# Adding and gating y in a selective scan: from GpSimd to VectorE, in halves

## The chip, the cores and the metric

The kernel runs on one core of a Trainium2 chip. Its engines are TensorE (PE; its weight loads are PEld), VectorE (DVE), ScalarE (ACT), GpSimd (POOL) and SyncE (SP, which only issues DMAs here). Each engine runs its own list of instructions in order, and waits on semaphores that other instructions raise. The metric is the device time of one launch in microseconds, as the median of several runs.

## The reference, cut to what matters

A block of a language model on 2048 tokens of width 512. The tokens are normalised, and the result goes through a Mamba2 scan and, beside it, through a top-2 mixture of eight experts; both are added to the input. What the change touches is the end of the scan:

```python
Y_off = jnp.einsum('bclgn,bcgHpn,bgHcl->bclgHp', Cc, prev, jnp.exp(dA_cs))
y = (Y_diag + Y_off).reshape(b, l, NHEADS, HEADDIM) + x * D_skip[None, None, :, None]
y = y.reshape(b, l, D_INNER)
y = y * jax.nn.silu(z)
yg = y.reshape(b, l, NGROUPS, D_INNER // NGROUPS)
yg = yg * jax.lax.rsqrt(jnp.mean(yg * yg, axis=-1, keepdims=True) + EPS)
y = yg.reshape(b, l, D_INNER) * norm_w
return y @ out_proj_w.T
```

`Y_diag` is what a tile of tokens gives itself, `Y_off` what the carried state gives it. `z` comes from the input projection, as `x`, `B` and `C` do (these through a convolution over four tokens).

## The kernel before

The scan works on T = 16 tiles of 128 tokens. The input projection works on G = 8 groups of two tiles and is cut into nine pairs of 128 columns (`stage(g, n)`), five that go through the convolution and four that make z. While the tiles t = 2g and 2g + 1 are scanned, the stages of group g + 1 are computed: four of them in the even tile, five in the odd one, placed by hand between the steps of the scan in the lists of TensorE, ScalarE and VectorE. All queues are written out by hand; what sets the order is the text of each engine's function, and semaphores tie them.

The steps that matter here, with the lines of the profile:

- TensorE, in a tile t: turns x into the banks `pxb` (L1601, behind `cadd`, the end of the adding of the states), a `stage`, C times B (L1608), in odd tiles `router(g + 2)` (L1438 to L1448), which computes scores and time steps of the group after next into bank `pxb[0]`, and so waits for `xdt_done` of the tile it stands in (L1442); a `stage`, `join`, then `project(t - 1)`, the output product of the tile before (L1523); then `off` (L1579, the carried state's part), `squares`, `diag` (L1586, the tile's own part), `states` (L1570), and further stages. A `stage` waits until the bank of the pair two stages before is free (`pair_free`).
- VectorE: xdt (L1282) from `pxb`, C times B masked (L1287), the decay kernel m (L1304), the convolution (L972) and its gate (L987), `decayed` (L1245: e2 becomes the carried part of y), `own` (L1255: y is the tile's own part and the skip), `carried` (L1275: the states are added to the carry), in even tiles `finish` (L1021: the output row), and the zs step (L978) of the z pairs, which also frees the pair's bank. The stages that are left at the end of a tile's list stand behind `carried` (L1363 to L1375). The zs step waits for ScalarE's tanh, and this for TensorE's stage.
- GpSimd: xdd (L516, from xdt), `sums` of the squares (L499 to L503), the decay of the carry (L528), `factor` (L508), and then for y of tiles 0 to 13: y plus e2 (L535, raises `yadd`; not in tile 0) and y times zs (L538, raises `ygate`), each over the whole tile, 128 partitions x 1024.
- In tiles 14 and 15 VectorE adds and gates y itself, in halves of 512 columns, inside `own` (L1259 to L1268, with `last_add` and `last_gate`).
- Who waits for `yadd`: SP's load of the next e2 (`load_decays2`). Who waits for `ygate`: TensorE's `project` and ScalarE's squares (L710).

The routing to the experts is computed in tiles 12 to 15 on VectorE (`choose`, `place_of`, `probabilities`, tables), and the experts follow the scan, from about 500 us on.

Of the kernel before, what the change touches and what calls it, by code (L numbers as in the profile page):

```python
# [11 lines left out]
ALU = mybir.AluOpType  # L12
# [9 lines left out]
P = 128  # L22
# [7 lines left out]
T = TOKENS // P  # L30
# [32 lines left out]
NX, NZ = CB // 2, XB // 2  # L63
# [34 lines left out]
def need(eng, semaphore, n):  # L98
    if n > 0:
        eng.wait_ge(semaphore, n)  # L100
# [21 lines left out]
def block(nc, x, w_in, w_dtr, w_out, conv_w_in, conv_b_in, dt_bias, a_log, d_skip_in, norm_w_in, w_gu, w_down, ident_in,  # L122
          tri_in, row_in, part_in, sel_in, tab_in, out):
    with ExitStack() as ctx:
        def sem(name):
            return ctx.enter_context(nc.semaphore(name))
# [51 lines left out]
        zs = [sb("zs0", [P, XB, GT])]  # L178
# [5 lines left out]
        y = sb("y", [P, XB, P])  # L184
# [8 lines left out]
        e2 = sb("e2", [P, XB, P])  # L193
# [92 lines left out]
        in_full, inx_free, inz_free, tz_done = sem("in_full"), sem("inx_free"), sem("inz_free"), sem("tz_done")  # L286
# [6 lines left out]
        e2_done, cbt, cbm_done, m_done, xdd_done = sem("e2_done"), sem("cbt"), sem("cbm_done"), sem("m_done"), sem("xdd_done")  # L293
        st, yoff, ydiag, ye, yd = sem("st"), sem("yoff"), sem("ydiag"), sem("ye"), sem("yd")
        cdec, cadd, yadd, ygate = sem("cdec"), sem("cadd"), sem("yadd"), sem("ygate")
        last_add, last_gate, ysqd, tree = sem("last_add"), sem("last_gate"), sem("ysqd"), sem("tree")
        op, ss, var_done, rstd_done = sem("op"), sem("ss"), sem("var_done"), sem("rstd_done")
        o_done, o_out, last_out = sem("o_done"), sem("o_out"), sem("last_out")

# [43 lines left out]
        def heads(vec, c):  # L343
            return vec[c][:, :].rearrange("p (a b) -> p b a", a=2).unsqueeze(3).broadcast_to([P, XB, 2, HD])
# [9 lines left out]
        def sync(sp):  # L354
# [18 lines left out]
                sp.dma_start(m[t % 2][:, :, :], cs_d[t].unsqueeze(0).broadcast_to([P, HEADS, P])).then_inc(bc_in[t % 2], 16)  # L373

            def load_decays2(t):
                if t < T - 1:
                    need(sp, yadd, t - 1)
                else:
                    sp.wait_ge(last_add, 2)
                for half in range(2):  # L380
                    sp.dma_start(e2[half * HD:(half + 1) * HD, :, :],
                                 cs_d[t][half * XB:(half + 1) * XB, :].unsqueeze(0).broadcast_to([HD, XB, P])
                                 ).then_inc(e2_in, 16)
# [37 lines left out]
            for t in range(T):  # L421
                g, c = t // 2, t % 2
# [57 lines left out]
        def gpsimd(pool):  # L480
            def root(q):
                pool.wait_ge(veps_done, q + 1)
                pool.tensor_tensor(rstdx[:, :], veps[:, :], nhalf[:, :], ALU.pow).then_inc(rstdx_done, 1)
# [13 lines left out]
            def sums(t):  # L497
                pool.wait_ge(ysqd, t + 1)
                pool.tensor_tensor(ysq[:, 0:4, :], ysq[:, 0:4, :], ysq[:, 4:8, :], ALU.add).then_inc(tree, 1)  # L499
                pool.wait_ge(tree, t * 3 + 1)  # L500
                pool.tensor_tensor(ysq[:, 0:2, :], ysq[:, 0:2, :], ysq[:, 2:4, :], ALU.add).then_inc(tree, 1)
                pool.wait_ge(tree, t * 3 + 2)
                pool.tensor_tensor(ysq[:, 0:1, :], ysq[:, 0:1, :], ysq[:, 1:2, :], ALU.add).then_inc(tree, 1)  # L503
# [6 lines left out]
            for t in range(T):  # L510
                g, c = t // 2, t % 2
                if t < T - 1:
                    pool.wait_ge(xdt_done, 2 * t + 2)
                    pool.wait_ge(dec_done, t + 1)
                    need(pool, st, t)
                    pool.tensor_tensor(xdd[:, :, :, :], xdt[:, :, :, :], heads(dec, c), ALU.mult).then_inc(xdd_done, 1)  # L516
                if c == 0 and g + 2 < G:
                    root(g + 2)
                if 0 < t < T - 2:
                    sums(t - 1)  # L520
                if t == T - 1:
                    factor(t - 1)
                if t == T - 1:
                    break
                if t:
                    pool.wait_ge(yoff, 2 * t)
                    pool.wait_ge(cadd, 2 * t)
                    pool.tensor_tensor(carry[:, :, :, :], carry[:, :, :, :], heads(cd, c), ALU.mult).then_inc(cdec, 1)  # L528
                    factor(t - 1)
                if t == T - 2:  # L530
                    continue
                pool.wait_ge(yd, 2 * t + 2)
                if t:
                    pool.wait_ge(ye, 2 * t)
                    pool.tensor_tensor(y[:, :, :], y[:, :, :], e2[:, :, :], ALU.add).then_inc(yadd, 1)  # L535
                    pool.wait_ge(yadd, t)
                pool.wait_ge(inz_free, NZ * (g + 1))
                pool.tensor_tensor(y[:, :, :], y[:, :, :], zs[g % 2][:, :, c * P:(c + 1) * P], ALU.mult).then_inc(ygate, 1)  # L538

            def gather(j):  # L540

# [82 lines left out]
        def scalar(act):  # L624
# [70 lines left out]
            def square(t):  # L695
                need(act, ss, t)
                if t == 0:
                    act.wait_ge(xn_out[0], 16)
                if t == T - 1:
                    for half in range(2):  # L700
                        act.wait_ge(last_gate, half + 3)
                        ins = act.activation(ysq[:, 4 * half:4 * half + 4, :], y[:, 4 * half:4 * half + 4, :],
                                             ACT.Square)
                    ins.then_inc(ysqd, 1)
                    return
                if t < T - 2:
                    act.wait_ge(ygate, t + 1)
                else:
                    act.wait_ge(last_gate, 2)
                act.activation(ysq[:, :, :], y[:, :, :], ACT.Square).then_inc(ysqd, 1)  # L710

            act.wait_ge(wr_in, 16)
# [41 lines left out]
            for t in range(T):  # L754
                g, c = t // 2, t % 2
# [104 lines left out]
        def vector(dve):  # L860
# [152 lines left out]
            def finish(t):  # L1013
                dve.wait_ge(rstd_done, t + 1)
                dve.wait_ge(op, t + 1)
                dve.wait_ge(res_in, 16 * (t + 1))
                if t:
                    dve.wait_ge(o_out, 16 * t)
                else:
                    dve.wait_ge(pad_out, 64)  # L1020
                dve.scalar_tensor_tensor(out=o[:, :], in0=po[:, :], scalar=rstd[:, 0:1], in1=res[:, :],  # L1021
                                         op0=ALU.mult, op1=ALU.add).then_inc(o_done, 1)
# [210 lines left out]
            for t in range(T):  # L1233
                g, c = t // 2, t % 2
                par = g % 2
                tok = slice(c * P, (c + 1) * P)
# [10 lines left out]
                def own(half):  # L1247
                    dve.wait_ge(ydiag, t * 2 + half + 1)
                    if half == 0:
                        need(dve, op, t)  # L1250
                        need(dve, ysqd, t)
                        if t == 0:
                            dve.wait_ge(xn_out[1], 16)
                    for b in range(4 * half, 4 * half + 4):
                        ins = dve.scalar_tensor_tensor(  # L1255
                            out=y[:, b, :], in0=xs[par][:, b, tok], scalar=d_skip[:, b:b + 1],
                            in1=py[1][:, b - 4 * half, :], op0=ALU.mult, op1=ALU.add)
                    ins.then_inc(yd, 1)
                    if t >= T - 2:  # L1259
                        blocks = slice(4 * half, 4 * half + 4)  # L1260
                        done = 2 * (t - T + 2) + half + 1
                        dve.wait_ge(yd, t * 2 + half + 1)
                        dve.wait_ge(ye, (t - 1) * 2 + half + 1)
                        dve.tensor_tensor(y[:, blocks, :], y[:, blocks, :], e2[:, blocks, :], ALU.add
                                          ).then_inc(last_add, 1)
                        dve.wait_ge(last_add, done)
                        dve.tensor_tensor(y[:, blocks, :], y[:, blocks, :], zs[par][:, blocks, tok], ALU.mult  # L1267
                                          ).then_inc(last_gate, 1)  # L1268

                def carried():  # L1270
                    dve.wait_ge(cdec, t)
# [90 lines left out]
                    break  # L1362
                if 0 < t < T - 2:  # L1363
                    carried()
                    if c == 0:
                        finish(t - 1)
                if t == T - 3:
                    probabilities()
                for n in taken[3:4]:
# [48 lines left out]
        def tensor(pe):  # L1418
# [93 lines left out]
                mm.then_inc(tok_done, 1)  # L1512

            def project(t):
                if t < T - 2:
                    pe.wait_ge(ygate, t + 1)
                need(pe, o_done, t)
                if t == 0:
                    pe.wait_ge(wo_done, XB)
                for b in range(XB):  # L1520
                    if t >= T - 2 and b % 4 == 0:
                        pe.wait_ge(last_gate, 2 * (t - T + 2) + b // 4 + 1)
                    mm = pe.matmul(po[:, :], y[:, b, :], wo[:, b, :], start=b == 0, stop=b == XB - 1)  # L1523
                mm.then_inc(op, 1)

# [30 lines left out]
            for t in range(T):  # L1556
                g, c = t // 2, t % 2
                par = g % 2
                tok = slice(c * P, (c + 1) * P)
# [270 lines left out]
```

## Time and profile before

| what | value |
|---|---|
| median of 3 runs | 690.48 us (688.75 to 691.83) |
| the profiled execution's own time | 691.86 us |
| its span in the profile | 689.9 us |
| TensorE busy | 641.2 us (93%) |
| VectorE busy | 504.3 us (73%) |
| ScalarE busy | 374.7 us (54%) |
| GpSimd busy | 295.8 us (43%) |
| mean granted clock of TensorE | 0.981 |
| chain of work that ended last | PE 60%, DVE 16%, issue 8%, DMA 7%, ACT 4%, POOL 3% |

Busy times are summed over the whole span, and so mix the scan with the experts. The scan's tiles begin with the turning of B (L1597): tile 0 at 49.0 us, tile 2 at 105.0, tile 9 at 247.1, tile 14 at 453.6; a pair of tiles takes 57.6 us in the steady part. What a wait costs is seen in the timeline (start, duration, engine and line; in brackets the idle time of the engine before it and what ended it), and the granted clock in the stretches (1.00 is 2.4 GHz, 0.50 is 1.2 GHz).

### The profile page before, as it was taken

How to read it: one execution, taken by the hardware profiler on the slowest of the kernel's cores; microseconds unless marked ns; L12 is line 12 of the kernel's file. 1: busy time of each engine (PE TensorE's matmuls, PEld its weight loads, DVE VectorE, ACT ScalarE, POOL GpSimd, SP SyncE). 2: the span in 40 equal slices, each digit the busy share in tenths (PEclk: the TensorE clock that was granted, in tenths of full speed). 3: DMA queues.
4: the chain of work that ended last, by engine and by line, in shares of the span. 5: the costliest groups of instructions: out<-in, count | busy, mean ns of one | idle time of the engine just before them, and what ended most of it. 6: DMA issues, size and time to landing. Idle time of an engine off the chain costs nothing.

```text
span 689.9 us, 12665 instructions
## 1 busy us (share of the span) xinstructions
PE 641.2 (93%) x4215; PEld 527.4 (76%) x4216; DVE 504.3 (73%) x1098; ACT 374.7 (54%) x787; POOL 295.8 (43%) x210
## 2 busy tenths in 40 slices
PE   4898799999999999999999989999798999999991
PEld 3897677878779777787877967677477888899981
DVE  6898677877977887787797788899976644444430
ACT  4778855563763755557376373638246444444441
POOL 2002235525354444553535425331327566656641
PEclk9999999999999999999999999999999999999997
DMA  8682014304222330420422203083866676667763
GB/s 263 218 311 96 1 32 153 103 22 153 72 83 81 104 124 31 153 102 23 153 69 86 97 29 130 1 281 108 271 210 98 119 123 122 122 119 124 127 98 46
DMA packets 31826, 80.38 MB, mean 117 GB/s; under 512 B 4768, under 2 KB 10016, under 8 KB 29600
## 3 DMA queue, kind: packets, MB, share of 16 engines
q1 hardware_dynamic: 22640, 57.97, 25.4%
q0 software_dynamic: 9136, 21.76, 17.3%
q8 instruction: 29, 0.48, 0.3%
q14 instruction: 21, 0.17, 0.1%
HBM read 59.93 MB, written 19.79 MB: 116 GB/s over the span
## 4 chain that ended last, share of the span: by engine, by line
PE 60%; DVE 16%; issue 8%; DMA 7%; ACT 4%; POOL 3%; SPq 1%; DVEq 0%; POOLq 0%; ACTq 0%
PE pi L1484 17%; PE po L1523 10%; PE pg L1705 10%; PE pd L1718 7%; DVE xs L972 5%; PE py L1586 3%; PE py L1579 3%; DMA m<-cs_d 2%; PE px L1688 2%; PE pxb L1570 2%; DVE y L1255 2%; PE pxb L1601 1%; DMA out<-yo,idx 1%; DVE xs L987 1%; PE phs L1728 1%
## 5 line engine op out<-in xcount | busy, mean ns | idle before, releaser
L1484 PE MATMUL pi<-xh,whl 128*128 128x256 f32 x1152 | 166.3, 287 | 1.8 <-DVE zs L978 1.3
L1484 PEld LDWEIGHTS pi<-xh,whl 128*128 128x128 f32 x1152 | 147.5, 190 | 4.6 <-issue 2.4
L972 DVE SCALAR_TENSOR_TENSOR xs<-raw,conv_w,xs 128x256 f32<-128x256 f32 x240 | 111.0, 527 | 12.1 <-ACT xs L664 12.0
L1523 PE MATMUL po<-wo,y 128*128 128x512 f32 x256 | 114.6, 601 | 0.4 <-DVE y L1267 0.4
L1484 PE MATMUL pi<-xl,whl 128*128 128x256 f32 x576 | 92.1, 282 | 0.0
L1523 PEld LDWEIGHTS po<-wo,y 128*128 128x128 f32 x256 | 48.0, 192 | 55.3 <-issue 55.1
L562 POOL DMA_INDIRECT out<-yo,idx x39 | 62.1, 1593 | 60.4 <-ACT yo L830 29.8
L689 ACT ACTIVATE m<-m,cs_tok 128x128 f32<-128x128 f32 x256 | 79.8, 390 | 0.5
L1484 PEld LDWEIGHTS pi<-xl,whl 128*128 128x128 f32 x576 | 78.9, 189 | 0.0
L1705 PE MATMUL pg<-ew,xgh 128*128 x312 | 65.1, 351 | 0.0
L528 POOL TENSOR_TENSOR carry<-carry,cd 128x1024 f32<-128x1024 f32 x14 | 27.5, 1967 | 81.9 <-PE py L1579 81.9
L667 ACT ACTIVATE zs<-pi 128x512 f32<-128x512 f32 x32 | 19.1, 597 | 73.2 <-PE pi L1484 73.2
L516 POOL TENSOR_TENSOR xdd<-xdt,dec 128x1024 f32<-128x1024 f32 x15 | 29.1, 1939 | 61.4 <-DVE xdt L1282 61.4
L1705 PEld LDWEIGHTS pg<-ew,xgh 128*128 128x128 f32 x312 | 53.3, 190 | 0.1
L535 POOL TENSOR_TENSOR y<-y,e 128x1024 f32<-128x1024 f32 x13 | 31.1, 2392 | 48.0 <-DVE y L1255 48.0
L549 POOL DMA_INDIRECT xg<-xn_d,idx x39 | 43.8, 1123 | 16.3 <-issue 4.7
L1397 DVE TENSOR_TENSOR hl<-phs,hh 96x256 fp32r<-96x256 f32 x39 | 16.4, 421 | 45.2 <-ACT hh L842 45.2
L830 ACT ACTIVATE yo<-pd,prob 128x512 f32<-128x512 f32 x39 | 26.9, 689 | 41.1 <-PE pd L1718 35.1
L1718 PE MATMUL pd<-ew,hh 96*128 x156 | 46.3, 419 | 1.7 <-DVE hl L1397 1.4
L1304 DVE TENSOR_TENSOR m<-m,cbm 128x2048 f32<-128x2048 f32 x16 | 46.5, 2908 | 0.8
L664 ACT ACTIVATE xs<-raw,conv_b,conv_w 128x256 f32<-128x256 f32 x80 | 43.8, 595 | 1.3
L499 POOL TENSOR_TENSOR ysq<-ysq 128x512 f32<-128x512 f32 x13 | 19.2, 1480 | 55.5 <-ACT ysq L710 55.5
(221 smaller groups left out, 1167.8 us busy)
## 6 DMA issues: line engine op xcount, KB each, us to landing
m<-cs_d SPq DMA_DIRECT2D x16, 1024.0 KB, 5.8
e<-cs_d SPq DMA_DIRECT2D x30, 256.0 KB, 4.4
ew<-in_w_gu SPq DMA_DIRECT2D x8, 768.0 KB, 7.9
w_as_read<-in_w_in SPq DMA_DIRECT2D x9, 512.0 KB, 8.9
res<-in_x SPq DMA_DIRECT2D x16, 256.0 KB, 3.8
out<-o SPq DMA_DIRECT2D x15, 256.0 KB
xin<-in_x SPq DMA_DIRECT2D x6, 512.0 KB, 3.9
xn_d<-xin SPq DMA_DIRECT2D x6, 512.0 KB, 2.8
```

The costliest lines, as they stand in the source:

```text
L516: pool.tensor_tensor(xdd[:, :, :, :], xdt[:, :, :, :], heads(dec, c), ALU.mult).then_inc(xdd_done, 1)
L535: pool.tensor_tensor(y[:, :, :], y[:, :, :], e2[:, :, :], ALU.add).then_inc(yadd, 1)
L549: pool.indirect_dma_start(to[j % 2][:, :], None, xn_d, bass.IndirectOffsetOnAxis(ap=idx[:, j:j + 1], axis=0)).then_inc(arrived[j % 2], 16)
L562: pool.indirect_dma_start(out, bass.IndirectOffsetOnAxis(ap=idx[:, j:j + 1], axis=0), yo[j % 2][:, :], None, compute_op=ALU.add).then_inc( ...
L664: act.activation(xs[par][:, b, :], raw[:, b, 0:GT], ACT.Identity, bias=conv_b[:, b:b + 1], scale=conv_w[:, b, 0:1]).then_inc(tap, 1)
L689: act.activation(m[c][:, hd, :], m[c][:, hd, :], ACT.Relu, bias=cs_tok[:, t % RING, hd:hd + 1], scale=-1.0).then_inc(seg, 1)
L972: dve.scalar_tensor_tensor(out=xs[par][:, b, :], in0=raw[:, b, k:k + GT], scalar=conv_w[:, b, k:k + 1], in1=xs[par][:, b, :], op0=ALU.mult ...
L1304: dve.tensor_tensor(m[c][:, :, :], m[c][:, :, :], cbm[:, :].unsqueeze(1).broadcast_to([P, HEADS, P]), ALU.mult).then_inc(m_done, 1)
L1484: mm = pe.matmul(bank[:, hf, :], whl[:, weight(g, n), lo, k, hf * P:(hf + 1) * P], xx[:, k, :], start=k3 == 0, stop=k3 == 11)
L1523: mm = pe.matmul(po[:, :], y[:, b, :], wo[:, b, :], start=b == 0, stop=b == XB - 1)
L1705: mm = pe.matmul(pg[par][:, 0:2 * F], xx[par][:, k, :], of(ww, e, k), start=n == 0, stop=n == 11)
L1718: mm = pe.matmul(pd[par][:, :], xx[par][:, k, :], of(ww, e, k), start=n == 0, stop=n == 5)
```

## The change

GpSimd no longer adds and gates y. VectorE does it in all tiles, in a new function `gate(half)`, which for one half of y waits for y and (but in tile 0) e2, adds, and multiplies by zs. In tiles 0 to 13 both halves are called behind `carried`, ahead of `finish` and of the stages left in the tile; in tiles 14 and 15 they are called inside `own` as before. The semaphores `last_add` and `last_gate` go; `yadd` and `ygate` count halves now, and those who wait for them (SP's load of e2, ScalarE's squares, TensorE's `project`, now by halves in all tiles) count along.

```diff
             def load_decays2(t):
-                if t < T - 1:
-                    need(sp, yadd, t - 1)
-                else:
-                    sp.wait_ge(last_add, 2)
+                need(sp, yadd, 2 * (t - 1))
...
                     factor(t - 1)
-                if t == T - 2:
-                    continue
-                pool.wait_ge(yd, 2 * t + 2)
-                if t:
-                    pool.wait_ge(ye, 2 * t)
-                    pool.tensor_tensor(y[:, :, :], y[:, :, :], e2[:, :, :], ALU.add).then_inc(yadd, 1)
-                    pool.wait_ge(yadd, t)
-                pool.wait_ge(inz_free, NZ * (g + 1))
-                pool.tensor_tensor(y[:, :, :], y[:, :, :], zs[g % 2][:, :, c * P:(c + 1) * P], ALU.mult).then_inc(ygate, 1)
...
-                if t < T - 2:
-                    act.wait_ge(ygate, t + 1)
-                else:
-                    act.wait_ge(last_gate, 2)
+                act.wait_ge(ygate, 2 * t + 2)
                 act.activation(ysq[:, :, :], y[:, :, :], ACT.Square).then_inc(ysqd, 1)
...
                     if t >= T - 2:
-                        blocks = slice(4 * half, 4 * half + 4)
-                        done = 2 * (t - T + 2) + half + 1
-                        dve.wait_ge(yd, t * 2 + half + 1)
+                        gate(half)
+
+                def gate(half):
+
+                    blocks = slice(4 * half, 4 * half + 4)
+                    dve.wait_ge(yd, t * 2 + half + 1)
+                    if t:
                         dve.wait_ge(ye, (t - 1) * 2 + half + 1)
                         dve.tensor_tensor(y[:, blocks, :], y[:, blocks, :], e2[:, blocks, :], ALU.add
-                                          ).then_inc(last_add, 1)
-                        dve.wait_ge(last_add, done)
-                        dve.tensor_tensor(y[:, blocks, :], y[:, blocks, :], zs[par][:, blocks, tok], ALU.mult
-                                          ).then_inc(last_gate, 1)
+                                          ).then_inc(yadd, 1)
+                        dve.wait_ge(yadd, 2 * (t - 1) + half + 1)
+                    dve.tensor_tensor(y[:, blocks, :], y[:, blocks, :], zs[par][:, blocks, tok], ALU.mult
+                                      ).then_inc(ygate, 1)
...
                 if 0 < t < T - 2:
                     carried()
-                    if c == 0:
-                        finish(t - 1)
+                if t < T - 2:
+                    gate(0)
+                    gate(1)
+                if 0 < t < T - 2 and c == 0:
+                    finish(t - 1)
...
             def project(t):
-                if t < T - 2:
-                    pe.wait_ge(ygate, t + 1)
                 need(pe, o_done, t)
...
                 for b in range(XB):
-                    if t >= T - 2 and b % 4 == 0:
-                        pe.wait_ge(last_gate, 2 * (t - T + 2) + b // 4 + 1)
+                    if b % 4 == 0:
+                        pe.wait_ge(ygate, 2 * t + b // 4 + 1)
                     mm = pe.matmul(po[:, :], y[:, b, :], wo[:, b, :], start=b == 0, stop=b == XB - 1)
```

## Rows read from the trace of the kernel before

**Rows 1.** Stretches, one pair: length, busy (xcount) PE PEld DVE ACT POOL, PEclk, DMA.

```profile
272.80:330.40 57.60, 57.17 (x402) 45.63 (x401) 46.88 (x109) 33.36 (x74) 26.95 (x17) 1.00 0.28 92
```

**Rows 2.** Instructions on tile y, on GpSimd: ns min/median/max, first and last start.

```profile
L538 POOL TENSOR_TENSOR y<-y,zs x14: 2372/2386/2758, 71.8 to 451.6; 128x1024 f32<-128x1024 f32 x14
L535 POOL TENSOR_TENSOR y<-y,e x13: 2383/2394/2399, 101.3 to 449.1; 128x1024 f32<-128x1024 f32 x13
```

**Rows 3.** Timeline, even to odd tile: start, us, instruction, [idle before <- releaser].

```profile
241.32 1.12 DVE L1255 SCALAR_TENSOR_TENSOR y<-xs,d_skip,py 128x128 f32<-128x128 f32 x4 [0.40 <-PE py L1586]
...
246.37 1.29 DVE L1275 TENSOR_TENSOR carry<-pxb,carry 128x512 f32<-128x512 f32 x2
...
248.82 0.69 DVE L987 SCALAR_TENSOR_TENSOR xs<-tx,xs 128x512 f32<-128x512 f32 x1
...
249.00 2.76 POOL L538 TENSOR_TENSOR y<-y,zs 128x1024 f32<-128x1024 f32 x1
249.43 1.29 DVE L1282 TENSOR_TENSOR xdt<-pxb,dt_tok 128x512 f32<-128x512 f32 x2
...
251.63 0.71 PE L1446 MATMUL pxb<-xh,wrs 128*48 128x256 f32 x4
...
252.31 3.50 DVE L1304 TENSOR_TENSOR m<-m,cbm 128x2048 f32<-128x2048 f32 x1
```

**Rows 4.** Timeline, VectorE in tile 14.

```profile
467.82 0.69 DVE L1264 TENSOR_TENSOR y<-y,e 128x512 f32<-128x512 f32 x1
...
468.55 0.69 DVE L1267 TENSOR_TENSOR y<-y,zs 128x512 f32<-128x512 f32 x1
469.16 0.15 DVE L1011 TENSOR_SCALAR var<-pk 128x1 f32<-128x1 f32 x1
```

**Rows 5.** Timeline, odd to even tile.

```profile
275.69 0.69 DVE L978 SCALAR_TENSOR_TENSOR zs<-zs,pi 128x512 f32<-128x512 f32 x1 [0.60 <-ACT zs L667]
...
278.55 0.69 DVE L978 SCALAR_TENSOR_TENSOR zs<-zs,pi 128x512 f32<-128x512 f32 x1 [2.16 <-ACT zs L667]
278.62 1.19 PE L1484 MATMUL pi<-xh,whl 128*128 128x256 f32 x8
```

**Rows 6.** Timeline, into tile 1, tile 13 and tile 14.

```profile
74.68 1.28 DVE L1282 TENSOR_TENSOR xdt<-pxb,dt_tok 128x512 f32<-128x512 f32 x2
...
77.40 0.72 PE L1446 MATMUL pxb<-xh,wrs 128*48 128x256 f32 x4
...
423.82 2.51 DVE L987 SCALAR_TENSOR_TENSOR xs<-tx,xs 128x512 f32<-128x512 f32 x1
...
427.67 0.22 PE L1493 MATMUL pxb<-picks,stri_b 128*128 128x136 bf16 x1 [1.05 <-DVE xdt L1282]
...
450.18 1.39 DVE L1109 TENSOR_SCALAR rt<-rt 128x16 f32<-128x16 f32 x1
...
451.89 2.15 DVE L1113 TENSOR_SCALAR pp<-rt 128x16 f32<-128x16 f32 x1
...
454.08 0.18 DVE L1115 TENSOR_TENSOR pp<-pp,rt 128x16 f32<-128x16 f32 x1
```

**Rows 7.** TensorE's long gaps (timeline), and stretches with PE busy, PEclk, DMA.

```profile
71.94 1.31 PE L1601 MATMUL pxb<-ident,xs 128*128 128x128 f32 x8 [2.05 <-ACT carry L808]
...
412.62 1.16 PE L1579 MATMUL py<-xs,carry 128*128 128x128 f32 x8 [1.83 <-DVE e L1245]
...
486.93 1.16 PE L1579 MATMUL py<-xs,carry 128*128 128x128 f32 x8 [1.64 <-DVE e L1245]
...
491.52 1.09 PE L1586 MATMUL py<-m,xdt 128*64 128x128 f32 x16 [2.41 <-DVE y L1255]
...
72.70:76.10 3.40, 3.40 (x19) 0.50 0.00 0
...
414.00:417.40 3.40, 3.40 (x18) 0.50 0.13 34
...
492.50:495.90 3.40, 2.95 (x7) 0.50 1.04 337
```

More of the change, by code:

```diff
@@ L295, in block @@
         cdec, cadd, yadd, ygate = sem("cdec"), sem("cadd"), sem("yadd"), sem("ygate")
-        last_add, last_gate, ysqd, tree = sem("last_add"), sem("last_gate"), sem("ysqd"), sem("tree")
+        ysqd, tree = sem("ysqd"), sem("tree")
         op, ss, var_done, rstd_done = sem("op"), sem("ss"), sem("var_done"), sem("rstd_done")
@@ L700, in square @@
                     for half in range(2):
-                        act.wait_ge(last_gate, half + 3)
+                        act.wait_ge(ygate, 2 * t + half + 1)
                         ins = act.activation(ysq[:, 4 * half:4 * half + 4, :], y[:, 4 * half:4 * half + 4, :],
```

## The prediction

> **What bounds the kernel now.** I read the busy time by stretches first. In a pair of scan tiles (57.60 us) TensorE is busy 57.17 us and VectorE 46.88 [rows 1]: TensorE has 0.4 us to spare in each pair, VectorE 10.7 us, GpSimd 30. So in the steady scan any microsecond for which TensorE has to wait is added to the end, and work that VectorE gains costs nothing only where it falls into a hole of VectorE that lies before the next thing TensorE needs. The share of busy time can't say that; the order in time at the two places where the new work goes in can. These I read next: the boundary from an even to an odd tile, and that from an odd to an even one. Last I looked at what the granted clock does after TensorE has stood still.
>
> **What is removed.** GpSimd's adding and gating of y take 2.39 us each, 13 and 14 times [rows 2]. The gated y is used by `project` one tile on, behind `router`, a `stage` and `join` in TensorE's order, and GpSimd had it at 249.00 + 2.76 = 251.76, when TensorE was only at `router` (251.63) [rows 3]. Nobody waited for it, so its removal gives nothing there, and having y some 2 us earlier gives nothing either.
> By the Trainium skill (GPSIMD Engine Reference, Engine selection) an elementwise step on a tile belongs on VectorE, since GpSimd takes about twice as long for two inputs. The rows agree on the cost (4.8 us against the 2.7 below), but by the order above the shorter path is worth 0 here, and the sum would stand as it is.
>
> **What is added.** Four VectorE instructions in a tile, of 128x512 each: add, multiply, add, multiply. Tile 14 has the same pair already: add at 467.82, multiply at 468.55 (0.73 later: it waits for the add), the next instruction at 469.16 (0.61 later) [rows 4]. So the block holds VectorE for 0.73 + 0.61 + 0.73 + 0.61 = 2.7 us (2.68; bounds: 4 x 0.61 = 2.4 with no wait showing, 4 x 0.73 = 2.9 with a wait on every step). It stands directly behind `carried`, ahead of `finish` (even tiles) and of what is left of `stage`. GpSimd isn't busy then, so nothing holds the block up. It happens in tiles 1 to 13, and tile 0 has the two multiplies alone.
>
> **Odd to even tile: hidden.** VectorE waits 0.60 us behind `carried` (from 275.09), runs the zs step of pair 7 (275.69), waits another 2.16 us and runs that of pair 8 (278.55) [rows 5]. The block goes from 275.0 to 277.7, pair 7 is then done at 277.7 + 0.69 = 278.4, and pair 8 starts at 278.5 as before. TensorE needs pair 7's bank for its next `stage` at 278.62 [rows 5]. So 2.76 us of holes take 2.7 us of work, with 0.2 us to spare: 0. If the block takes longer than that it shows here one to one; at 0.2 us over, six boundaries (after tiles 1, 3, 5, 7, 9, 11) cost 1.2 us. That cover is thin and is my upper bound's first term.
>
> **Even to odd tile: not hidden.** Here VectorE has no hole: `carried` ends at 246.37 + 1.29 = 247.66, and `finish`, zs, the gated conv step (248.82) and xdt (249.43 to 250.72) follow without a gap [rows 3]. With the block in front xdt ends at 250.72 + 2.70 = 253.4. Who waits for xdt? In odd tiles `router(g + 2)` writes to the bank that xdt reads, and so waits for both halves of xdt of this very tile (L1442). TensorE reaches it at 251.63, only 0.9 us after xdt is done now [rows 3]. Queued behind it on TensorE is everything else. The new wait is 253.42 + 0.1 (for the semaphore) - 251.63 = 1.9 us. The pattern stands in front of tiles 3, 5, 7, 9 and 11, five times, with the same slack. It comes back each time, since VectorE is in step with TensorE again by then: `own(0)` waits 0.40 us for TensorE's product in steady tiles [rows 3]. 5 x 1.92 = 9.6 us; with the bounds of the block 5 x 1.6 = 8 to 5 x 2.1 = 10.5.
>
> **The other tiles.** Tile 0 to 1: the two multiplies add 1.3 us, but GpSimd's gate goes, and with it the stretching of the gated conv step; TensorE reaches `router` at 77.40, xdt starts at 74.68 [rows 6]: 0. Tile 12 to 13: the conv step L987 takes 2.51 us beside GpSimd's gate, and 0.69 where no gate is in its way [rows 3, 6]; 1.8 us of it go and 2.7 come, so TensorE's wait for xdt (1.05 us now, L1493) grows by at most 0.9 us; I take half of that, since VectorE also waits there now [rows 6]. Tile 13 to 14: L1109 and L1113, on 16 columns, take 1.39 and 2.15 us beside GpSimd, where L1115 on as many takes 0.18 [rows 6]; 3.2 us go, 2.7 come: 0.5 us earlier, in a part where VectorE sets the pace. Together 0 within 0.5 us.
> The carried part's load on the SP queue waits for `yadd`, now behind the second add (0.7 us later at an even to odd boundary). Behind it queue `store` and `load_res`. ScalarE's use of e2 follows the load by over 4 us and feeds `join`, which itself comes 1.9 us later than before: 0.
>
> **The clock.** While TensorE waits its clock may fall. It was granted at 0.50 (1.2 of 2.4 GHz) from 414.0 to 417.4, right after a gap of 1.83 us; gaps of 2.05 and 2.41 us were followed by the same, one of 1.64 us was not [rows 7]. A stretch of 3.4 us at half speed does 1.7 us of full-speed work: 1.7 us lost each. The new gaps of 1.9 us lie among those that mostly brought a fall, but none in the steady part shows whether they do; the bounds are no fall (0) and five (8.5 us). I take three, as three of the four such gaps did: 5.1 us.
>
> **Sum.** 9.6 + 5.1 + 0 = 14.7 us. On the profiled execution (691.86 us with a span of 689.9) that makes 706.6; on the median of the runs, 690.48, which is 1.4 us below it, 705.2 us.
>
> **The rivals.**
> (a) The waits come, but the clock holds (no fall or one). For it: 1.9 us is close to the 1.64 that brought none. Then 690.5 + 9.6 = 700.1, or 701.8 with one.
> (b) All falls come, and the odd to even cover of 0.2 us gives way. 690.5 + 9.6 + 8.5 + 1.2 = 709.8; with the block at 2.9 us another 1: 711.
> (c) Not slower: GpSimd's gate has been holding VectorE up, and what VectorE gets back pays for the block. Its place is between `carried` and xdt at the even to odd boundary; it decides once at least 1.8 of the 2.7 us come back there, because then the 0.9 us of slack covers the rest. For it: the 2.51, 1.39 and 2.15 us above [rows 6]. Against it: in the steady boundary L987 starts before GpSimd's gate and takes 0.69 us, and it is GpSimd that is late (2.76 us instead of 2.39) [rows 2, 3]. The one instruction that is stretched in steady tiles is L1304 (3.50 us, beside GpSimd's xdd, which starts as soon as xdt and the gate are done) [rows 3], and xdd moves with xdt, so they still meet. Price if it held: 5 x 1.9 us gone, no new gaps, so 690.5 + 0 = 690.5 us.
> The Trainium skill (SBUF — State Buffer, Who interferes with whom) has the rule for it: a VectorE instruction with two SBUF inputs and a GpSimd instruction that reads SBUF exclude one another for the whole instruction. The rows on L987 fit; by the rule alone the change would free VectorE, and at this boundary the order in time shows that there is nothing to free.
> (d) Faster: the 0.5 us that the probabilities give back in tile 13, and more such in the tail where VectorE sets the pace, without the new waits. It can't exceed the 3.2 us that L1109 and L1113 lose now: 690.5 - 3.2 = 687.3 us.
>
> **How the numbers follow.** Forecast, two to four falls (703.5 to 706.9 us): 0.50. (a) 0.23. (b) 0.19. (c) 0.06. (d) 0.02. The likeliest is 705.2 us. The range leaves (c), (d) and the upper half of (b) out: 699 to 710.5 us. A measurement of this kernel tells about 0.5% (3.5 us) from no change; (d) is 0.02 faster, (c) 0.06 the same, and all the rest slower, 0.92.
>
> **What the changed profile would show.** TensorE's first matmul of `router` (L1446) waiting 1.9 us for VectorE's xdt in five odd tiles, and in no tile 1; the pair of tiles at 59.5 us and 61.2 with a fall of the clock; granted clock of 0.50 in about three more stretches, each right behind such a wait; no wait of TensorE before the first `stage` of an even tile; four y instructions within 2.7 us behind each `carried`; GpSimd some 65 us less busy (27 x 2.39). The prediction is wrong if `router` doesn't wait (then xdt came sooner than the block allows, or TensorE later), if the block takes visibly more than 2.7 us, or if VectorE loses time at another place that TensorE waits for, such as `decayed` or `own`.

## The result

| | before | after |
|---|---|---|
| median, first comparison | 690.8 us | 696.88 us (696.7 to 697.36) |
| ratio, with its 95% interval | | 1.0106 (1.007 to 1.0143) |
| median, second comparison (below, after2) | 690.38 us | 699.23 us (697.79 to 702.23) |
| ratio, with its 95% interval | | 1.0142 (1.0113 to 1.0172) |
| span of the profiled execution (first) | 689.9 us | 694.9 us |
| mean granted clock in it | 0.981 | 0.990 |

The change makes the kernel slower, by 6 us in the first comparison and by 9 to 10 us in the second (8.9 by the medians, 9.8 by the ratio). The forecast was 705.2 us with a range from 699 to 710.5; the first measurement lies 2 us below the range.

The busy times of the changed kernel, from the first part of its page (engine, busy us, share, instructions):

```profile
PE 635.4 (91%) x4215; PEld 521.9 (75%) x4216; DVE 533.7 (77%) x1152; ACT 374.2 (54%) x787; POOL 227.5 (33%) x183
```

GpSimd has 68 us less, VectorE only 29 us more, for 54 instructions of 0.69 us (37 us, each taken alone). Part of the difference is stretching beside GpSimd that went: the gated conv step has 27.2 us in its 40 instructions instead of 31.0, and L1109 and L1113 have 3.2 us less. Against that the decay kernel m has 49.0 us instead of 46.5. The rest wasn't traced to instructions. In a pair of tiles (stretch and length, then busy time and instructions of PE, PEld, DVE, ACT, POOL, then the granted clock) TensorE does what it did [rows 1], over a longer time:

```profile
225.90:285.10 59.20, 57.21 (x402) 45.60 (x401) 52.11 (x117) 33.21 (x74) 16.95 (x14) 1.00 0.27 89
```

Where it stands still is told by the waits of TensorE in the changed kernel (waiting instruction, what released it, us in total, times, longest):

```profile
PE pxb L1438 <- DVE xdt L1271: 8.2, 5, 1.6
...
PE pxb L1591 <- DVE carry L1264: 2.9, 7, 0.8
PE py L1569 <- DVE e L1230: 2.5, 2, 1.8
```

L1438 is `router` (L1446 before) and L1271 is xdt (L1282 before). It is a new group, and it is the largest one in the scan. The boundary from tile 4 to 5 in the timeline of the changed kernel answers to [rows 3], which is the same boundary from tile 6 to 7 (247.1 us, given above as the start of tile 9, is that of tile 7; tile 9 starts at 304.8):

```profile
188.96 0.68 DVE L1253 TENSOR_TENSOR y<-y,e 128x512 f32<-128x512 f32 x1
...
189.67 0.69 DVE L1256 TENSOR_TENSOR y<-y,zs 128x512 f32<-128x512 f32 x1
...
190.28 0.69 DVE L1253 TENSOR_TENSOR y<-y,e 128x512 f32<-128x512 f32 x1
...
191.00 0.69 DVE L1256 TENSOR_TENSOR y<-y,zs 128x512 f32<-128x512 f32 x1
...
191.60 0.75 DVE L1006 SCALAR_TENSOR_TENSOR o<-po,rstdy,res 128x512 f32<-128x512 f32 x1
...
192.86 0.69 DVE L972 SCALAR_TENSOR_TENSOR xs<-tx,xs 128x512 f32<-128x512 f32 x1
192.87 0.39 PE L1598 MATMUL pk<-xs 128*128 128x128 f32 x2
...
193.46 1.28 DVE L1271 TENSOR_TENSOR xdt<-pxb,dt_tok 128x512 f32<-128x512 f32 x2
...
194.89 0.64 PE L1438 MATMUL pxb<-xh,wrs 128*48 128x256 f32 x4 [1.64 <-DVE xdt L1271]
195.05 3.87 DVE L1293 TENSOR_TENSOR m<-m,cbm 128x2048 f32<-128x2048 f32 x1
```

The block takes 191.60 - 188.96 = 2.64 us, xdt ends at 194.74, and TensorE's `router` starts 0.15 us later with 1.64 us of idle time before it. The same stands before tiles 3, 7, 9 and 11. At the other boundary, odd to even, nothing waits, as in [rows 5]:

```profile
220.85 0.68 DVE L963 SCALAR_TENSOR_TENSOR zs<-zs,pi 128x512 f32<-128x512 f32 x1
...
221.74 0.69 DVE L963 SCALAR_TENSOR_TENSOR zs<-zs,pi 128x512 f32<-128x512 f32 x1 [0.21 <-ACT zs L655]
221.81 1.19 PE L1476 MATMUL pi<-xh,whl 128*128 128x256 f32 x8
```

Of the 2.76 us of holes 0.21 us is left.

### The profile page after: what moved, and what is told of

It is laid out like the page before. It is cut to its first block, busy times and chain, and to the rows that moved or that the text cites. A ratio compares the mean times of both kernels' runs of the same rounds, so it can differ in the third digit from the quotient of the medians.

```text
span 694.9 us, 12691 instructions
## 1 busy us (share of the span) xinstructions
PE 635.4 (91%) x4215; PEld 521.9 (75%) x4216; DVE 533.7 (77%) x1152; ACT 374.2 (54%) x787; POOL 227.5 (33%) x183
## 4 chain that ended last, share of the span: by engine, by line
PE 65%; DVE 18%; DMA 5%; issue 5%; ACT 3%; SPq 2%; POOL 1%; DVEq 0%; ACTq 0%; POOLq 0%
PE pi L1476 18%; PE po L1513 13%; PE pg L1695 10%; PE pd L1708 7%; DVE xs L957 5%; PE py L1569 4%; PE py L1576 3%; PE pxb L1560 2%; DVE y L1240 2%; DMA out<-yo,idx 2%; PE px L1678 2%; DVE xs L972 1%; DVE y L1253 1%; DVE carry L1264 1%; DMA out<-o 1%
## 5 line engine op out<-in xcount | busy, mean ns | idle before, releaser
L1513 PE MATMUL po<-wo,y 128*128 128x512 f32 x256 | 113.2, 595 | 0.4 <-DVE y L1256 0.4
L525 POOL TENSOR_TENSOR carry<-carry,cd 128x1024 f32<-128x1024 f32 x14 | 27.2, 1944 | 83.3 <-PE py L1569 83.3
L1389 DVE TENSOR_TENSOR hl<-phs,hh 96x256 fp32r<-96x256 f32 x39 | 16.4, 421 | 46.5 <-ACT hh L827 46.5
L1293 DVE TENSOR_TENSOR m<-m,cbm 128x2048 f32<-128x2048 f32 x16 | 49.0, 3066 | 0.8
L1380 DVE SCALAR_TENSOR_TENSOR hg<-th,pg 128x192 f32<-128x192 f32 x39 | 13.8, 353 | 36.2 <-ACT th L821 33.9
L1240 DVE SCALAR_TENSOR_TENSOR y<-xs,d_skip,py 128x128 f32<-128x128 f32 x128 | 35.8, 340 | 5.9 <-PE py L1576 5.7
```

The lines of the kernel that those rows point to most:

```text
L1240: ins = dve.scalar_tensor_tensor(out=y[:, b, :], in0=xs[par][:, b, tok], scalar=d_skip[:, b:b + 1], in1=py[1][:, b - 4 * half, :], op0=ALU ...
L1293: dve.tensor_tensor(m[c][:, :, :], m[c][:, :, :], cbm[:, :].unsqueeze(1).broadcast_to([P, HEADS, P]), ALU.mult).then_inc(m_done, 1)
```

## The experiments

Two theories were set against each other. W: the cost is TensorE's wait for xdt at `router` in five odd tiles, and nothing else. R: VectorE is later everywhere with 37 us more work, and the cost goes with the number of tiles moved. Beside that the clock had to be settled.

**One half of the change at a time.** In `dve_odd` and `dve_even` GpSimd keeps y in the tiles of the other parity (the condition of `dve_odd` is shown, that of `dve_even` has `== 0`):

```diff
-                if t < T - 2:
+                if t < T - 2 and t % 2 == 1:
                     gate(0)
                     gate(1)
```

> VectorE adds and gates y in the odd tiles (1 to 13) alone, GpSimd in the even ones. Theory W (the cost is TensorE's wait for xdt in router, behind even to odd boundaries): no such wait, as in the kernel before; 690.8 us within 1.5. Rival R (VectorE is later everywhere with 37 us more work, so the cost goes with the number of tiles moved): about half of the 6.1 us, 693.8 us.

> VectorE adds and gates y in the even tiles (0 to 12) alone, GpSimd in the odd ones. Theory W: the whole cost, five gaps of 1.6 us at router and one in tile 13: 697 us within 1.5. Rival R: half of it, 693.8 us.

Measured: `dve_odd` 689.27 us against 689.62 for the kernel before, ratio 0.9999 (0.9967 to 1.0032); `dve_even` 696.76 us, ratio 1.0137 (1.0084 to 1.0189). One half costs nothing, the other half all of it. R falls in this form: nearly as many instructions were added in both (28 in the odd tiles, 26 in the even ones). The waits of TensorE in `dve_even` are those of the changed kernel:

```profile
PE pxb L1448 <- DVE xdt L1281: 8.2, 5, 1.6
```

and `dve_odd` has none at `router`.

**The same work in another order.** `split` keeps all of it on VectorE and moves the multiplies and `finish` of even tiles behind the next xdt. Where lines are left out below, the first place has the two adds alone, the second the two multiplies of tile t - 1:

```diff
-                if t < T - 2:
+                if t < T - 2 and (c == 1 or t == 0):
                     gate(0)
                     gate(1)
-                if 0 < t < T - 2 and c == 0:
-                    finish(t - 1)
+                elif t < T - 2:
...
                         .unsqueeze(3).broadcast_to([P, 4, 2, HD]), ALU.mult).then_inc(xdt_done, 1)
+                if c == 1 and 1 < t < T - 1:
...
+                    finish(t - 2)
                 dve.wait_ge(cbt, t + 1)
```

> The changed kernel, but in even tiles 2 to 12 only the adds stand behind carried; the multiplies and finish come behind the next tile's xdt. xdt is then 1.2 - 0.7 = 0.5 us later than in the kernel before, within its 0.9 us of slack. Theory W: no gap at router, tile 13 included or down to 1 us: 688 us within 1.5. Rival R (the same work on VectorE, as late): 697 us.

Measured: 688.61 us against 689.62, ratio 0.9985 (0.9961 to 1.0009). The timeline of `split` at the boundary from tile 4 to 5:

```profile
186.58 1.29 DVE L1369 TENSOR_TENSOR y<-y,e 128x512 f32<-128x512 f32 x2
...
188.98 1.28 DVE L1271 TENSOR_TENSOR xdt<-pxb,dt_tok 128x512 f32<-128x512 f32 x2
190.18 1.28 DVE L1279 TENSOR_TENSOR y<-y,zs 128x512 f32<-128x512 f32 x2
```

```profile
190.65 0.72 PE L1450 MATMUL pxb<-xh,wrs 128*48 128x256 f32 x4
```

xdt ends at 190.26, 0.4 us ahead of `router`, and there is no gap. So 54 instructions more on VectorE cost nothing, once those that stand in front of xdt fit into the slack. This version isn't measurably faster than the kernel before either. It isn't free of waits: late in tile 13 TensorE waits 2.09 us for VectorE at `off`, where it waits 0.67 in the kernel before.

**The bank that makes `router` wait.** `after_po` is the changed kernel with `router`'s rows in another bank:

```diff
-            return bank[0:2 * C, 0:GT], bank[:, GT:GT + 2 * C]
+            return (po if q > 1 else bank)[0:2 * C, 0:GT], bank[:, GT:GT + 2 * C]
...
             def router(q):
-                if q >= 2:
-                    pe.wait_ge(xdt_done, 2 * (2 * (q - 2) + 1) + 2)
+                if q > 2:
+                    pe.wait_ge(o_done, 2 * (q - 2))
...
             def join(q):
+                if q >= 2:
+                    pe.wait_ge(xdt_done, 2 * (2 * (q - 2) + 1) + 2)
```

> The changed kernel, but from group 2 on router writes its rows to bank po (free since finish) instead of the bank that xdt reads; join waits for xdt in its place, 4 us later. Theory W: the five gaps go, 5 x 1.66 = 8.3 us less than 696.9, so 688.6 us, below the kernel before by what its clock falls cost; the gap in tile 13 stays. Rival R: VectorE is as late as before, the wait turns up at the next step that needs VectorE: 697 us.

> Control for after_po: the kernel before with router's rows in bank po, where nothing waits for xdt at router. Both theories: no change, within 1.5 us of the kernel before, and no gap where after_po had new ones (the second diag of odd tiles, the first stage of even tiles). If the 0.76 us gaps appear here too, they come from the new bank and not from VectorE being late.

Measured: `after_po` 696.47 us, ratio 1.0107 (1.0087 to 1.0127), and in a second run of it (`after_po2`, below) 694.58 us, 1.0069 (1.0043 to 1.0095). `before_po` 690.1 us against 690.38, ratio 1.0005 (0.9981 to 1.0028): no cost of the bank itself is measurable. The five gaps at `router` are gone, but W's 688.6 us isn't reached. R's 697 us is, in the first run: its count of moved tiles was refuted by the halves, but what it said here, that the wait turns up at the next step that needs VectorE, is what happened. What came instead, in the timeline of `after_po` in tile 3:

```profile
149.72 2.28 DVE L925 SCALAR_TENSOR_TENSOR step_acc<-step_acc,step_s 128x32 f32<-128x32 f32 x3
...
150.02 1.93 POOL L525 TENSOR_TENSOR carry<-carry,cd 128x1024 f32<-128x1024 f32 x1 [4.93 <-PE py L1571]
...
152.59 1.11 DVE L1240 SCALAR_TENSOR_TENSOR y<-xs,d_skip,py 128x128 f32<-128x128 f32 x4
...
153.76 1.09 PE L1578 MATMUL py<-m,xdt 128*64 128x128 f32 x16 [0.76 <-DVE y L1240]
```

Three small steps that take 0.64 us elsewhere take 2.28 here, all of it by the third of them; the longest of the 42 such instructions in the trace took 1877 ns, the longest in the changed kernel 193 ns. TensorE doesn't wait for VectorE at `router` any more, so xdt ends 1.73 us behind the start of `router` instead of 0.92 us ahead of it as in the kernel before. At the small steps VectorE is still 0.8 us later than there (0.5 in tile 3), and the third starts 0.16 us after GpSimd has started on the carry. In tile 7 of the same execution it starts 0.01 us ahead of GpSimd, and isn't stretched:

```profile
267.10 0.65 DVE L925 SCALAR_TENSOR_TENSOR step_acc<-step_acc,step_s 128x32 f32<-128x32 f32 x3
...
267.56 1.98 POOL L525 TENSOR_TENSOR carry<-carry,cd 128x1024 f32<-128x1024 f32 x1 [5.10 <-PE py L1571]
```

The gap of 0.76 us is missing there too, and from this `router` to the next it takes 57.78 us, where the three other pairs take 58.67 to 58.68. The Trainium skill's rule from the forecast (SBUF — State Buffer, Who interferes with whom: the two exclude one another for a whole instruction) fits the rows of tile 3: both instructions read two inputs from SBUF. `po_steps` moves just these three steps:

```diff
-                    time_steps(g + 2, 0, 10)
+                    time_steps(g + 2, 0, 7)
...
-                    time_steps(g + 2, 10, 14)
+                    time_steps(g + 2, 7, 14)
```

> after_po, with three small VectorE steps (L925 on 128x32, two SBUF inputs) moved from ahead of decayed(1) in odd tiles to behind finish. In after_po one of them stood still for 1.8 us in four of five odd tiles, just as GpSimd's decay of the carry began, and TensorE then waited 0.76 us at the second diag and 0.24 us at the next stage. Theory P (VectorE, no longer held at router, runs late into GpSimd's carry step, and the two exclude one another): the stretch and both gaps go, 4 to 5 us below after_po, 691 to 692.5 us. Rival Q (VectorE is simply late by its added work, the stretch only coincides): the 0.76 us gaps stay, less than 1 us below after_po.

> after_po again, beside po_steps on the same chip: 696.5 us within 1.5 under both theories.

Measured: `po_steps` 693.66 us (693.46 without one run at 700.18), ratio 1.0058 (1.0037 to 1.008), beside 694.58 us for `after_po2`. P had set 4 to 5 us less, Q less than 1. The first of the following rows is of `po_steps` (line, engine, ns min/median/max), the second of `after_po2`:

```profile
L925 DVE SCALAR_TENSOR_TENSOR step_acc<-step_acc,step_s x42: 178/192/194, 99.3 to 390.3; 128x32 f32<-128x32 f32 x42
```

```profile
L925 DVE SCALAR_TENSOR_TENSOR step_acc<-step_acc,step_s x42: 174/192/1943, 94.1 to 393.6; 128x32 f32<-128x32 f32 x42
```

The stretch and the five gaps of 0.76 us are gone in `po_steps`, as theory P said, and its span is 690.9 us against 694.7. But in the medians only 0.9 to 1.1 us shows, nearer to Q's number than to P's. Gaps of 0.30 us before the first stage of even tiles and of 1.63 us in tile 13 (L1487) are still there. So this is shown: a later VectorE runs into GpSimd, and that makes TensorE wait. Its price is seen in the pairs: 57.9 us from `router` to `router` in `po_steps`, 58.7 in `after_po2`, which with tile 7 above makes 0.8 to 0.9 us a pair. Why the medians show less than five such pairs is open.

**The clock, by dose.** `dose1` and `dose2` put one or two more instructions of 128x512 (the maximum of y with itself) into the block of even tiles 2 to 10. The condition of `dose1` is shown, that of `dose2` has `half < 2`:

```diff
                         dve.wait_ge(yadd, 2 * (t - 1) + half + 1)
+                        if c == 0 and t < T - 4 and half < 1:
+                            dve.tensor_tensor(y[:, blocks, :], y[:, blocks, :], y[:, blocks, :], ALU.max
+                                              ).then_inc(again, 1)
+                            dve.wait_ge(again, 1 * (t // 2 - 1) + half + 1)
```

> The changed kernel again, beside the kernel before on one chip. If its cost is what the waits add up to in the profile (five times 1.66 us, and 1.1 in tile 13, so 9.4 us) and the 6.1 us first measured were chance in how often the clock fell, it comes 8 to 9.5 us above the kernel before, ratio 1.012 to 1.014. If the clock falls less in the changed kernel for a reason of its own, the ratio stays at 1.009 and its profile has one fall of the clock between 60 and 500 us again, where that of before had four.

> The changed kernel with one more VectorE instruction (y = max(y, y) on half 0, 0.73 us) between add and multiply in even tiles 2 to 10, so the gaps of TensorE at router go from 1.64 to about 2.4 us. If a fall of the clock goes with the length of the gap, two or three of the five gaps bring one (1.7 us each): 3.7 + 3.4 to 5.1 us above the changed kernel. If gaps at router bring none whatever their length: 3.7 us above it.

> The same with two such instructions (1.46 us), gaps of about 3.1 us. If falls go with the length, three to five of the five gaps bring one: 7.3 + 5 to 8.5 us above the changed kernel. If not: 7.3 us above it.

| | gap at `router`, five times | falls behind these gaps | median | ratio to before |
|---|---|---|---|---|
| after2 | 1.64 us | 0 | 699.23 us | 1.0142 (1.0113 to 1.0172) |
| dose1 | 2.36 us | 5 | 708.78 us | 1.0272 (1.0222 to 1.0321) |
| dose2 | 3.08 us | 5 | 717.1 us | 1.0393 (1.0352 to 1.0433) |

The gaps of one execution differ by up to 0.02 us. In `dose2` three of the five falls begin before the gap has ended, and one lasts 6.8 us instead of 3.4. Both doses cost more than was expected even if falls go with the length (7.1 to 8.8 and 12.3 to 15.8 us above the changed kernel).

The first gap of `dose1`, then four stretches of it (length, PE busy, granted clock): one that begins with the gap, and those right behind the first, the third and the fourth gap.

```profile
139.65 0.64 PE L1442 MATMUL pxb<-xh,wrs 128*48 128x256 f32 x4 [2.36 <-DVE xdt L1275]
```

```profile
137.30:140.70 3.40, 1.05 (x9) 1.00 0.97 290
140.70:144.10 3.40, 3.40 (x19) 0.50 0.02 7
...
263.60:267.00 3.40, 3.40 (x19) 0.50 0.03 10
325.00:328.40 3.40, 3.40 (x19) 0.51 0.08 31
```

The same two stretches at the first gap of `after2`:

```profile
138.90:142.30 3.40, 1.79 (x16) 1.00 0.71 214
142.30:145.70 3.40, 3.40 (x25) 1.00 0.00 0
```

0.73 us more of gap costs 3.6 us by itself and 9.6 us measured; the other 6 us go with the clock. Two more instructions cost 7.2 us by themselves and 17.9 us measured. That gaps bring no fall at `router` whatever their length is excluded; that a gap of 1.64 us brings one has no case in 15 (three profiles: the changed kernel, `dve_even`, `after2`). The five falls of `dose1` are those of one execution, with its gaps at nearly equal distances (61.4 to 61.8 us), and so not five independent cases. The profiled run took 711.31 us at a mean granted clock of 0.967; two of the other three took 706.25 and 705.51 us at 0.979 and 0.977, and so must have had fewer falls.

Nor does the length of a gap decide by itself. A gap of 2.05 us stands before tile 1 in all twelve profiles; a fall follows it in seven and none in five. A gap of 1.47 us at `join` in tile 1 is followed by one in `after2` and `dose1`, and the fall at 468.6 us in the kernel before has no gap of even 1 us beside it. What else decides stays open. The falls that the kernel had before show the same. The gap of 1.83 us in tile 12 is in both profiles of the changed kernel, and only in one of them does the clock fall behind it. The changed kernel, first profile (the gap, and the stretch behind it):

```profile
418.50 1.16 PE L1569 MATMUL py<-xs,carry 128*128 128x128 f32 x8 [1.83 <-DVE e L1230]
```

```profile
418.50:421.90 3.40, 3.40 (x29) 1.00 0.16 47
```

`after2`:

```profile
423.99 1.16 PE L1569 MATMUL py<-xs,carry 128*128 128x128 f32 x8 [1.83 <-DVE e L1230]
```

```profile
425.40:428.80 3.40, 3.40 (x19) 0.51 0.08 23
```

**The steady tiles alone.** From the start of tile 2 to that of tile 12 no clock falls in any profile but those of the doses, so the waits can be seen there without it (one execution each):

| | tiles 2 to 12, us | falls of the clock in them |
|---|---|---|
| before, before_po | 287.76, 288.92 | 0 |
| dve_odd, split | 287.42, 287.35 | 0 |
| after, after2, dve_even | 296.08, 296.80, 296.43 | 0 |
| after_po, after_po2 | 292.07, 293.07 | 0 |
| po_steps | 289.67 | 0 |
| dose1 | 307.57 | 5 |
| dose2 | 312.09 | 5, one of double length |

Moving `router` to another bank thus took back 3 to 5 of the 8 to 9 us here, and moving the three small steps 2.4 to 3.4 more. `dose1` needs 10.8 us more than `after2`: 3.6 for the gaps and 7.2 for five falls, 1.4 us each.

## Why the prediction was wrong

**Right.** The bound (TensorE in the steady scan), the place (`router` waits for xdt of its own tile), the number (five, none in tile 1), the hidden boundary (odd to even, 0.21 us to spare where 0.2 was forecast), and the length of the block (2.64 us for 2.7). L1109 and L1113 take 0.17 us each once GpSimd is silent. Rival (c) was right in that GpSimd had held VectorE up (6.9 us at the conv step, L1109 and L1113), and wrong at the place where it had to: the gated conv step before xdt takes 0.69 us in both kernels, and L1304 takes longer than before, 3.87 us instead of 3.50.

**The waits: 9.6 us forecast, 8 to 9 measured.** TensorE's `router` comes 194.89 - 192.87 = 2.02 us after the product before it, where it came 0.14 us after it (251.63, [rows 3], and the following line of the kernel before): 1.88 us, as the forecast's 1.9.

```profile
251.49 0.39 PE L1608 MATMUL pk<-xs 128*128 128x128 f32 x2
```

But the pair grew by less. From the first to the last `router` behind such a gap the changed kernel needs 59.2 us a pair and `after2` 59.4, against 57.6: 1.6 to 1.8 us each. Some 0.1 to 0.3 us of each wait comes back within the pair. By which instruction was not looked into. The 0.1 us that the sum has for the semaphore stands in no row; between the end of xdt and `router` 0.15 us were measured.

**Tiles 12 and 13: 0 within 0.5 us forecast, 0.1 or 1.7 measured.** With a fall in tile 12 they take 60.85 us in the kernel before and 60.99 in `after2`. With none they take 58.61 (`before_po`) and 58.62 (`dve_odd`), but 60.32 in the changed kernel and 60.33 in `dve_even`. In tile 13 TensorE then waits 1.63 us for xdt, at a step where no wait is seen in the first two. The forecast read its 1.05 us from an execution with a fall.

**The clock: 5.1 us forecast, 0 behind these gaps.** This is the step that failed: the term for falls behind the new gaps. Its three falls of 1.7 us were none in all three profiles with these gaps (0 of 15). The forecast said that the new gaps of 1.9 us "lie among those that mostly brought a fall". The 1.9 us are by how much `router` starts later; the numbers they were compared with, 1.64 to 2.41 us, are idle times as the trace shows them. The trace has the end of the product before at 193.26 (192.87 + 0.39), though in the kernel before the next starts 0.14 us after such a product's start; so the same wait stands there as 1.64 us. And the one gap of 1.64 us in [rows 7] had brought no fall. Read on one scale, the forecast's own rows pointed to rival (a) with no fall, 700.1 us, though by a single gap; the second comparison gave 699.23. That the scale was mixed is shown. Why gaps of 1.64 us brought no fall isn't, since the length doesn't decide alone.

**The rest of the 14.7 us.** The first comparison has 6.1 us where the waits alone come to 8 to 9. In its profile the clock fell once between 57 and 515 us; in the profile of the kernel before it fell four times, in that of `after2` five times. What one costs is seen from tile 0 to tile 2: 54.5 to 54.7 us without a fall, 56.1 to 56.3 with one, 57.7 and 57.9 with two. In single runs time and clock go together: `after2` took 697.79 us at a mean granted clock of 0.988 and 702.23 at 0.979, and the kernel before took from 685.92 to 693.79 us in the same comparison. The four runs of the first comparison were at 0.986 to 0.990. Runs of like clock compare better: among those at 0.986 to 0.988 the kernel before took 688.1 us in the mean (four runs of the second comparison), the changed kernel 697.0 (three of the first) and 698.1 (two of the second), so 9 to 10 us more in both. The first value, 6.1 us, is then 3 to 4 us low by chance in how often the clock fell. The second (8.9 us by medians, 9.8 by the ratio) agrees with the sum of the waits. That the changed kernel falls less often for a reason of its own, which after2 was run for, finds no support; with ten runs of it in all it isn't excluded either.

**One claim was too strong.** The forecast had VectorE "in step with TensorE again" within the odd tile, by the 0.40 us for which `own(0)` waits. That holds because TensorE itself stands still at `router`. With that wait removed (`after_po`) VectorE's lateness lives on through the tile and turns into other waits.

## What to carry to other kernels

Adding work to an engine that is 73% busy is free or costly by where it stands: look for the next thing that the bounding engine takes from it, and for holes ahead of that; in `split` the same 54 instructions in another order cost nothing. A wait removed at one place comes back at the next if the late engine is still late. Compare a wait that is worked out from start times with waits that a trace shows only after putting both on one scale. And where the clock falls in some executions and not in others, compare stretches without a fall, or runs of like mean clock, before reading a cost from medians.

## What the runs showed of the hardware that wasn't expected

- Behind a gap of 1.64 us the granted clock never fell at `router` (0 of 15 in three executions); around one of 2.36 us it fell five times of five in one execution, and around 3.08 us too. There 0.73 us more in each of five gaps cost 9.6 us in the medians instead of 3.6.
- The length of a gap doesn't tell whether the clock falls: the one of 2.05 us before tile 1 brought a fall in seven of twelve executions, one of 1.47 us in two. So a kernel with such gaps varies by itself: from 685.92 us at a mean granted clock of 0.988 to 693.79 at 0.979 for the kernel before in one comparison.
- A small VectorE instruction can wait for a GpSimd instruction that started before it: 128x32 took 1.88 us instead of 0.19 beside the 1.93 us step on the carry. Where it started 0.01 us ahead of that step it took 0.20 us.
